# A six-layer attention stack: softmax work of layer 0 spread over slots, layer 1's projection started at the copies, the last slots laid out anew, and two layers' context matmuls in high and low halves

## What is computed

```python
# layer 0: 8 heads of 32
q, k, v = x @ Wq + bq, x @ Wk + bk, x @ Wv + bv
attn = softmax(where(adj == 0, -inf, q k^T / sqrt(32)))
x = layernorm(attn v @ Wo + bo + x) * gamma + beta
# layer 1: one head of 256
attn = softmax(where(adj == 0, -inf, (x Wq)(x Wk)^T / 16))
x = layernorm(x + (attn (x Wv)) @ Wo + bo) * gamma + beta
# layers 2 to 5: one head of 128
q, k = x Wq^T + bq, x Wk^T + bk
attn = softmax(where(adj == 0, -1e10, q k^T / sqrt(128)))
x = layernorm(x + (attn x) Wc^T) * gamma + beta
```

## Time and profile before

| what | value |
|---|---|
| median of 3 runs | 2371.49 us (2371.39 to 2374.79) |
| the profiled execution's own time | 2373.87 us |
| its span in the trace | 2372.1 us |
| PE busy | 2259.9 us, 95% |
| PE weight loads busy | 2136.2 us, 90% |
| DVE busy | 1783.3 us, 75% |
| ACT busy | 1620.0 us, 68% |
| POOL busy | 1794.9 us, 76% |
| granted PE clock, mean over the span | 0.99 of full speed |

### The profile page before, as it was taken

The page is one execution under the profiler, slowest core; times in us unless marked ns, Lnnn a source line. Parts: engine busy times, 40 slices in busy tenths (PEclk is TensorE's granted clock), DMA queues, the critical chain, the costliest instruction groups (busy, mean ns, idle before and its releaser), DMA issues.

```text
span 2372.1 us, 59576 instructions
## 1 busy us (share of the span) xinstructions
PE 2259.9 (95%) x20624; PEld 2136.2 (90%) x20624; DVE 1783.3 (75%) x7734; ACT 1620.0 (68%) x5515; POOL 1794.9 (76%) x2399
## 2 busy tenths in 40 slices
PE   6899999999999999999999999999999999999985
PEld 5799999999999999999999999999999999999974
DVE  4777777777877877877877877877777777777864
ACT  5667767767767767767767767766766766767742
POOL 3368878878878878878878878878878878878751
PEclk9999999999999999999999999999999999999998
DMA  4000000100110000010010000000010010000000
GB/s 154 20 23 24 30 28 24 30 28 25 29 28 25 29 28 26 28 28 26 28 28 27 27 28 28 26 28 28 26 28 28 26 28 28 26 29 17 15 10 14
DMA packets 38747, 68.78 MB, mean 29 GB/s; under 512 B 4400, under 2 KB 12848, under 8 KB 37936
## 3 DMA queue, kind: packets, MB, share of 16 engines
q1 hardware_dynamic: 38448, 64.97, 9.0%
HBM read 48.18 MB, written 16.78 MB: 27 GB/s over the span
## 4 chain that ended last, share of the span: by engine, by line
PE 80%; DVE 9%; ACT 7%; issue 2%; POOL 1%; DMA 0%; POOLq 0%; SPq 0%; DVEq 0%
PE value_bank L450 17%; PE qk_bank L442 16%; PE context_bank L595 9%; PE unit_bank L450 7%; PE unit_bank L442 7%; PE qk_bank L549 7%; PE score_bank L579 5%; ACT probs L676 5%; PE unit_bank L506 4%; PE unit_bank L518 3%; DVE scores L820 2%; PE score_bank L576 2%; PE score_bank L586 2%; DVE xT_lo L854 2%; DVE scores L860 1%
## 5 line engine op out<-in xcount | busy, mean ns | idle before, releaser
L1046 POOL TENSOR_TENSOR x<-y,rows 128x512 f32<-128x512 f32 x305 | 392.0, 1285 | 188.9 <-DVE y L913 188.9
L698 ACT CAST xT_hi<-qk_bank 128x512 fp32r<-128x512 f32 x320 | 187.7, 587 | 399.8 <-PE qk_bank L549 399.6
L676 ACT ACTIVATE probs<-scores,negmax 128x128 f32<-128x128 f32 x1024 | 399.1, 393 | 88.6 <-DVE negmax L820 88.6
L913 DVE TENSOR_SCALAR y<-y,mv,rstd 128x256 f32<-128x256 f32 x730 | 304.2, 459 | 191.6 <-POOL rstd L1030 191.3
L442 PE MATMUL qk_bank<-xT_hi,w_lo 128*128 128x256 f32 x1280 | 411.5, 321 | 21.6 <-DVE xT_lo L854 21.3
L1054 POOL TENSOR_TENSOR x<-x,rows 128x512 f32<-128x512 f32 x305 | 393.8, 1291 | 19.2
L450 PE MATMUL value_bank<-w_lo,xT_hi 128*128 128x256 f32 x1280 | 394.4, 308 | 0.0
L442 PE MATMUL qk_bank<-xT_lo,w_hi 128*128 128x256 f32 x1280 | 363.5, 284 | 0.0
L442 PE MATMUL qk_bank<-xT_hi,w_hi 128*128 128x256 f32 x1280 | 362.1, 283 | 0.0
L450 PE MATMUL value_bank<-w_hi,xT_lo 128*128 128x256 f32 x1280 | 361.8, 283 | 0.0
L450 PE MATMUL value_bank<-w_hi,xT_hi 128*128 128x256 f32 x1280 | 361.0, 282 | 0.0
(11 more groups left out here) (93 smaller groups left out, 6503.3 us busy)
## 6 DMA issues: line engine op xcount, KB each, us to landing
x0T<-xT_in SPq DMA_DIRECT2D x64, 256.0 KB, 3.0
x<-x_in SPq DMA_DIRECT2D x64, 256.0 KB, 3.0
out<-x_out SPq DMA_DIRECT2D x64, 256.0 KB, 2.3
adj<-adj_in SPq DMA_DIRECT2D x64, 128.0 KB, 2.2
late_weights<-w_in SPq DMA_DIRECT2D x2, 1024.0 KB, 7.1
rows<-rows_in SPq DMA_DIRECT2D x1, 1792.0 KB, 11.7
probs0T<-w_in SPq DMA_DIRECT2D x4, 256.0 KB, 4.2
x<-w_in SPq DMA_DIRECT2D x1, 1024.0 KB, 13.2
```

Of the source, the lines that this page charges most:

```text
L676: e = act.activation(probs0[:, j, g, quad], scores0[:, j, g, quad], ACT.Exp, scale=-1.0, bias=negmax0[:, j, g, quad:quad + 1], accum_out=t ...
L913: m = dve.tensor_scalar(y[:, r, g], y[:, r, g], mv[:, r, g, 0:1], rstd[:, r, g:g + 1], ALU.subtract, ALU.mult)
L1046: pool.tensor_tensor(result(norm), y[:, NORM_AT[norm] % YS], row_of_each(f"gamma{layer}"), ALU.mult).then_inc(zg_ready, 1)
```

## The change

1. Exponentials: unit 0's four activations are split, the first graph's before `move_qk` in phase 4, the second's after `move_probsT`. Unit 2 moves from the end of phase 0 to where unit 3 was in phase 1, unit 3 to the end of phase 1. DVE's `reciprocal0` and `row_max0(3)` move with them. POOL's and PE's orders stay.
2. Layer 1's projection has its own function: the eight products with `xT_hi` start once ACT's two copies are done, the four with `xT_lo` come last. They overwrite `qk_bank`, so `split_lo` of layer 1 reads `xT` in SBUF instead of `qk_bank`. It keeps its place in DVE's order except for three items at the end.
3. Layers 4 and 5: ACT writes `v_hi` and `probsT_hi`, DVE computes `v_lo` and `probsT_lo` (new `split_v`, 128x512, and `split_probsT`, 128x256), and the context is three fast products for each graph. PE waits for the low halves, before it reads them and before it overwrites `value_bank` and `score_bank`.
4. The last group's layers 3, 4 and 5 go from slots 323, 327, 331 to 322, 325, 328; group 62's layers 4 and 5 to 324 and 327. In slots 321, 324 and 327 DVE does `split_lo` later in its order.

```diff
-MOVED = {LAST_FIRST + 11: LAST_FIRST + 13}
+MOVED = {LAST_FIRST + 7: LAST_FIRST + 9, LAST_FIRST + 8: LAST_FIRST + 7, LAST_FIRST + 11: LAST_FIRST + 12,
+         LAST_FIRST + 12: LAST_FIRST + 10, LAST_FIRST + 16: LAST_FIRST + 13}
+FILL_IN = [LAST_FIRST + 6, LAST_FIRST + 9, LAST_FIRST + 12]
...
+def in_halves(i):
+    return item(i)[0] >= LAYERS - 2
...
+            def project_fused(i):
+                hi, lo = xT_hi[:, ring(i)], xT_lo[:, ring(i)]
+                pe.wait_ge(xT_ready, group + 1)
+                for n in range(KD):
+                    for kd in range(KD):
+                        for w in (w_lo, w_hi):
+                            pe.matmul(qk_bank[:, n * G * N:(n + 1) * G * N], split(w, "scores1", kd, n * P, n * P + P),
+                                      flat(hi[:, kd]), start=n == 0 and kd == 0 and w is w_lo, stop=False)
+                pe.wait_ge(xT_lo_ready, after(i))
+                for n in range(KD):
+                    for kd in range(KD):
+                        mm = pe.matmul(qk_bank[:, n * G * N:(n + 1) * G * N], split(w_hi, "scores1", kd, n * P, n * P + P),
+                                       flat(lo[:, kd]), start=False, stop=n == KD - 1 and kd == KD - 1)
...
             def context(i):
-                pe.wait_ge(probsT_ready, after(i))
-                pe.wait_ge(v_ready, after(i))
+                wait_probsT_moved(i)
+                wait_values_moved(i)
...
+                    for left, right in ((probsT_hi, v_lo), (probsT_hi, v_hi), (probsT_lo, v_hi)):
+                        mm = pe.matmul(context_bank[:, g * D:(g + 1) * D], left[:, ring(i), g], right[:, ring(i), g],
+                                       start=right is v_lo, stop=left is probsT_lo)
```

ACT's loop over the slots:

```diff
                 if (group := due(i, 6)) is not None:
-                    exp0(group, 0)
+                    exp0(group, 0, [0])
                 if (group := due(i, 5)) is not None:
                     exp0(group, 1)
                 if (group := due(i, 4)) is not None:
                     move_probs0T(group, 1)
-                    exp0(group, 3)
+                    exp0(group, 2)
...
                 if item(i - 1):
                     move_probsT(i - 1)
-                if (group := due(i, 5)) is not None:
-                    exp0(group, 2)
+                if (group := due(i, 6)) is not None:
+                    exp0(group, 0, [1])
+                if (group := due(i, 4)) is not None:
+                    exp0(group, 3)
```

DVE's functions and its loop over the slots:

```diff
             def split_lo(i):
+                source = qk_bank[:, :]
                 if layer == 1:
                     dve.wait_ge(xT_ready, group + 1)
+                    source = flat3(xT[:, :])
...
+            def split_probsT(i):
+                dve.wait_ge(probsT_hi_ready, IN_HALVES_AT[i] + 1)
+                dve.tensor_tensor(flat(probsT_lo[:, ring(i)]), score_bank[:, 0:G * N],
+                                  flat(probsT_hi[:, ring(i)]).bitcast(F32), ALU.subtract).then_inc(probsT_lo_ready, 1)
...
                 if item(i - 1):
                     row_max(i - 1)
-                if item(i):
+                if item(i) and not fills_in(i):
                     split_lo(i)
...
+                if item(i - 1) and in_halves(i - 1):
+                    split_v(i - 1)
...
-                if (group := due(i, 4)) is not None:
-                    reciprocal0(group, 2)
+                if (group := due(i, 3)) is not None:
+                    reciprocal0(group, 3)
...
+                if (group := due(i, 4)) is not None:
+                    reciprocal0(group, 2)
                     row_max0(group, 3)
...
                 if item(i - 2):
                     finish_or_normalise(("item", i - 2))
+                if item(i - 1) and in_halves(i - 1):
+                    split_probsT(i - 1)
                 if (group := due(i, 2)) is not None:
                     add_residual(("group", group))
```

More of the change, by code:

```diff
@@ L61, with fills_in @@
 LAST_FIRST = PERIOD * (GROUPS - 1)
-MOVED = {LAST_FIRST + 11: LAST_FIRST + 13}
+MOVED = {LAST_FIRST + 7: LAST_FIRST + 9, LAST_FIRST + 8: LAST_FIRST + 7, LAST_FIRST + 11: LAST_FIRST + 12,
+         LAST_FIRST + 12: LAST_FIRST + 10, LAST_FIRST + 16: LAST_FIRST + 13}
+PLACED = {slot: regular for regular, slot in MOVED.items()}
+FILL_IN = [LAST_FIRST + 6, LAST_FIRST + 9, LAST_FIRST + 12]
+def fills_in(i):
+    return i in FILL_IN
 def item(i):
-    if i in MOVED:
+    if i in MOVED and i not in PLACED:
         return None
-    for start, moved in MOVED.items():
-        i = start if i == moved else i
+    i = PLACED.get(i, i)
     layer = 1 if i % PERIOD == 0 else LAYERS - i % PERIOD
@@ L140 @@
 LATER_LEAD = 3
+def in_halves(i):
+    return item(i)[0] >= LAYERS - 2
+IN_HALVES_AT = {i: at for at, i in enumerate(i for i in ITEMS if in_halves(i))}
+IN_FULL_AT = {i: at for at, i in enumerate(i for i in ITEMS if not in_halves(i))}
 KEPT = [i for i in ITEMS if item(i)[0] > 1]
@@ L205, in gnn_stack @@
         v = sb("v", [RING, G, D])
+        v_hi = sb("v_hi", [RING, G, D], F32R)
+        v_lo = sb("v_lo", [RING, G, D], F32R)
+        probsT_hi = sb("probsT_hi", [RING, G, N], F32R)
+        probsT_lo = sb("probsT_lo", [RING, G, N], F32R)
         scores = sb("scores", [RING, G, N])
@@ L283, in gnn_stack @@
         v_ready = sem("v_ready")
+        v_hi_ready = sem("v_hi_ready")
+        v_lo_ready = sem("v_lo_ready")
         scores_in_psum = sem("scores_in_psum")
@@ L554, in project_qk, with wait_values_moved, wait_probsT_moved @@
                 layer, group = item(i)
-                parts = [("scores1", 0), ("scores1", P)] if layer == 1 else [(f"wqT{layer}", 0), (f"wkT{layer}", 0)]
                 pe.wait_ge(xT_lo_ready, after(i))
-                project(qk_bank, xT_hi[:, ring(i)], xT_lo[:, ring(i)], parts).then_inc(qk_in_psum, 1)
+                project(qk_bank, xT_hi[:, ring(i)], xT_lo[:, ring(i)],
+                        [(f"wqT{layer}", 0), (f"wkT{layer}", 0)]).then_inc(qk_in_psum, 1)
+            def project_fused(i):
+                layer, group = item(i)
+                hi, lo = xT_hi[:, ring(i)], xT_lo[:, ring(i)]
[10 more added lines that the diff above has]
+                                       flat(lo[:, kd]), start=False, stop=n == KD - 1 and kd == KD - 1)
+                mm.then_inc(qk_in_psum, 1)
+            def wait_values_moved(i):
+                if in_halves(i):
+                    pe.wait_ge(v_lo_ready, IN_HALVES_AT[i] + 1)
+                else:
+                    pe.wait_ge(v_ready, IN_FULL_AT[i] + 1)
+            def wait_probsT_moved(i):
+                if in_halves(i):
+                    pe.wait_ge(probsT_lo_ready, IN_HALVES_AT[i] + 1)
+                else:
+                    pe.wait_ge(probsT_ready, IN_FULL_AT[i] + 1)
             def project_v(i, g):
@@ L617, in _ @@
                     context(i - 2)
-                if item(i):
+                if item(i) and item(i)[0] == 1:
+                    project_fused(i)
+                elif item(i):
                     project_qk(i)
@@ L670, in move_k0, with exp0 @@
                 m.then_inc(k0_ready, 1)
-            def exp0(group, j):
+            def exp0(group, j, graphs=range(G)):
                 act.wait_ge(negmax0_ready, after_unit(group, j))
-                for g in range(G):
+                for g in graphs:
                     for quad in range(QUADS):
@@ L715, in move_v @@
                 act.wait_ge(v_in_psum, after(i))
-                act.copy(flat(v[:, ring(i)]), value_bank[:, :]).then_inc(v_ready, 1)
+                if NTH[i] >= RING:
+                    act.wait_ge(context_in_psum, after(i) - RING)
+                if in_halves(i):
+                    act.copy(flat(v_hi[:, ring(i)]), value_bank[:, :]).then_inc(v_hi_ready, 1)
+                else:
+                    act.copy(flat(v[:, ring(i)]), value_bank[:, :]).then_inc(v_ready, 1)
             def softmax(i):
@@ L726, in move_probsT @@
                 act.wait_ge(probsT_in_psum, after(i))
-                act.copy(flat(probsT[:, ring(i)]), score_bank[:, 0:G * N]).then_inc(probsT_ready, 1)
+                if in_halves(i):
+                    act.copy(flat(probsT_hi[:, ring(i)]), score_bank[:, 0:G * N]).then_inc(probsT_hi_ready, 1)
+                else:
+                    act.copy(flat(probsT[:, ring(i)]), score_bank[:, 0:G * N]).then_inc(probsT_ready, 1)
             def split_first(name):
@@ L976, in _ @@
                     reciprocal_total(i - 1)
+                if i + 1 == FILL_IN[0]:
+                    split_lo(i + 1)
+                if i in FILL_IN[1:]:
+                    split_lo(i)
                 if (group := due(i, 6)) is not None:
@@ L985, in _ @@
                     find_valid(group)
-                    reciprocal0(group, 3)
                 if (group := due(i, 8)) is not None:
```

21 lines of the change are left out of this document (15 added, 6 removed).

## The result

| what | before | after |
|---|---|---|
| median | 2372.53 us (2371.39 to 2374.79, 4 runs) | 2424.12 us (2423.15 to 2425.3, 4 runs) |
| span of the profiled execution | 2372.1 us | 2421.1 us |
| PE busy | 2259.9 us, 95% | 2254.6 us, 93% |
| DVE busy | 1783.3 us, 75% | 1945.4 us, 80% |
| a period in the middle, from phase 3 to phase 3 | 35.55 us | 36.35 us |

The ratio is 1.0216 with a 95% interval of 1.0199 to 1.0234: the changed kernel is 2.2% slower. 2415 had been forecast. Two executions stand far from the rest and are unexplained: one of ten of the kernel before beside the new end alone took 2405.23 us at a granted clock of 0.923, and one of seven of the new end alone took 12561.91 us and enters no ratio.

What follows compares the result with a forecast made beforehand. The prediction took the kernel as balanced between PE's chain and a DVE and POOL chain of nearly equal length. Periods +43.5, ramp +1.2, end -2 made +43 us, so 2415 us; forecast range 2395 to 2432 (0.60), stated range 2364 to 2432.

Steps and rivals of the forecast that it cites:

- The chain through DVE and POOL: Phase 3: split_v (+0.1) and split_probsT (0.38) on DVE make the layer-0 result on POOL 0.48 us later.
- The context in halves: PE, layers 4 and 5: six fast products replace a full context, gaining 0.13 to 0.16 us, twice a period.
- Exponentials, inside the whole change: Layer 1's transpose_x stops waiting for kT, waits for the layer-0 result, and gains 0.12 us, not 0.79.
- The collision: Layer 1's split_lo, both operands in SBUF, waits for POOL's scale; unit 0's normalisation starts 1.03 us later.
- PE at unit 1: PE's transposes of unit 1's probabilities wait for POOL and start 0.94 us later.
- Given back in phase 1: Context and twelve products in phase 1 no longer meet a late split_lo: 0.19 us a period back.
- The sum: Middle periods: +0.94 - 0.19 = +0.75 us each, bounds 0.6 to 1.0; 58 periods give +43.5.
- Ramp: First groups: later unit 2 exponential and unit 3 maximum cost about 1.2 us once, bounds 0 to 5.
- End: Last group: about +2 us for layers 4 and 5 each, -2 for each of three layers; -2, bounds -8 to +3.
- One reasoned step: At unit 1's transposes, POOL only 0.14 us ahead: a PE gain before them brings at most 0.1.
- Rival (b): POOL's chain has slack and PE's time counts: up to 1.1 us a period saved, 2307 or 2340; chance 0.17.
- the 0.21: Context in halves: gain if three passes replace four, a quarter off; the prediction went by the row's 0.15 instead.

Runs made afterwards that it cites:

- the new end alone: The kernel before with only the new slots at the end (MOVED, FILL_IN and the late split_lo): 2368.56 us, ratio 0.9962 (0.9922 to 1.0002).

## Why the prediction was right, and where it was not

The forecast was the likeliest case and its mechanism is what the runs show. It put the whole at +43 us; the profiled executions differ by 49. Point by point:

- **The chain through DVE and POOL.** Right. From the context at 1216.51, `shift` of the layer-0 result ends at 11.35 (1226.58 + 1.28); before it was 10.95. Forecast +0.48, measured 0.41 on average. `split_probsT` was put at 0.38 between bounds of 0.31 and 0.44: the next operation starts 0.34 after it, and it takes 0.42.
- **The context in halves.** Context and the twelve products behind it take 1218.66 − 1216.51 = 2.15, 2.27 before: 0.12, and 0.13 on average, against 0.13 to 0.16.
- **Exponentials, inside the whole change.** `transpose_x` was put 0.12 earlier and waiting for `x`: it waits for `x`, and is 0.19 earlier.
- **The collision.** Right in kind, place and size: `scale` over the split, 1.57 in the period shown, an end 0.55 after POOL's; unit 0 of layer 0 starts 0.96 later, 1.03 was forecast. POOL's wait for the reciprocal: 0.71 against 0.7.
- **PE at unit 1.** 0.88 later, against 0.94. Both are a little smaller than forecast because `scale`, behind which the split ends, is 0.41 later on average and not 0.48.
- **Given back in phase 1.** Right in place, mis-sized: context and products take 1239.21 − 1236.92 = 2.29 instead of 2.46, so 0.17 came back there. But ahead of it the transposes, which now follow POOL, take 1236.92 − 1236.43 = 0.49 instead of 0.43, and 0.11 is left; 0.19 was forecast. This miss and the one before it, 0.08 and 0.06, have opposite signs in the sum and cancel.
- **The sum.** +0.80 a period against +0.75. The forecast's 35.60 + 0.75 = 36.35 is what was measured, though partly by luck: the one period it started from was one of the longer ones, and the mean is 35.55. 57 periods at 0.80 are 45.5.
- **Ramp.** Not confirmed: +1.2 forecast, −0.9 measured, and two executions of the same ramp differ by 0.8 at other granted clocks, so one pair of executions cannot show it.
- **End.** Wrong: −2 forecast, bounds −8 to +3; measured +4.3, of which 1.7 are the two longer periods. The new slots alone gave −5.7. The halves alone cost 10.9 in the old end; with new slots they cost 8 to 10 (after's 186.8 or the 186.6 without the projection, against 176.8 for the slots alone). The two terms fared differently. "−2 for each of three layers", −6, is about what the new slots give, though no run shows whether for the reasons stated. "+2 for layers 4 and 5 each", +4, was really 8 to 10. Layer 5 alone costs 4.4 in the old end. Where the rest goes is in part argued: the one place shown costs 1.8, and an item in halves stands behind a neighbour's normalise in more places than the last group's.

One reasoned step fell, though the sum stood. The prediction said that a gain on PE's side before the unit-1 transposes can bring at most 0.1, since POOL was only 0.14 ahead. The exponentials alone brought 0.33 a period. The 0.14 was read rightly; wrong was to treat POOL's time as fixed. Part of its chain waits for PE a slot earlier, so both moved: layer 1's split on DVE stands ahead of PE's projection as well as of POOL's unit 0. That PE passes unit 1's transposes without waiting for POOL would have said that PE's own path had the last word there. In the whole change this does not show, because the halves lengthen the chain that `x` comes by, and the blocked split lies behind it. Rival (b), that PE's time counts, was right in part: alone, the exponentials brought 0.33 of the 0.6 that PE's side had to give, and with layer 5's halves 0.52. What stopped it there was not POOL's lead but the normalise and the row maximum ahead of the split on DVE.

The parts do not add. One by one, in us a period: exponentials −0.33, halves +0.38, early projection +0.35, which is +0.40; together +0.80. (By the medians the parts are −21.1, +33.3, +25.4 and −5.4 for the new end, 32.2 us of the 51.6; the rest is 0.34 a period.) The traces show where it comes from. As long as layer 1 projects in the old order, the period follows the start of that projection, which waits for `xT_lo`: counted from the phase-3 context 14.13 before, 13.79 with the exponentials, 13.62 with layer 5's halves as well, 14.58 with both layers' halves, 14.67 with the split reading `xT`, for periods of 35.55, 35.23, 35.03, 35.94 and 36.09. With the early projection it follows POOL instead. PE's unit-1 transposes, counted from the context in phase 3, come at 19.07 before; at 18.73 with the exponentials and at 18.57 with layer 5's halves as well; at 19.53 with the projection, and at 19.37 with the projection, exponentials and layer 5's halves. So, if beside the projection layer 5's halves are still worth their 0.16, the exponentials are worth nothing: their 0.34 came by way of an earlier `kT`, `xT` and split, and with the projection the split ends 0.55 after POOL's `scale` whenever its input is there; `scale` itself starts at 12.79 with the exponentials as without. That alone is most of the 0.40. It is worked out and not measured: exponentials and projection without any halves were not run.

## What to carry to other kernels

Before giving an instruction on DVE a second operand in SBUF, look at what POOL does at that very moment in the timeline. The price is not the instruction's but the rest of POOL's, and then whatever is queued behind it on DVE. Where two chains run within 0.2 us of each other, take the changes apart: here the exponentials were worth 0.33 us a period and layer 5's halves 0.20, and layer 4's halves and the projection took 0.55 and 0.76 away again (the projection by itself 0.35), in one change that was read as one. And do not take an engine's lead as fixed: follow it back to what set it.

## What the runs showed of the hardware

- The blocking works in both directions: DVE's 0.69 split becomes 1.2 to 1.57 when POOL's 128x512 operation has begun before it, and in all middle periods of the five kernels with it ends 0.54 to 0.55 after POOL's, whether it began 0.25 or 0.6 after it; when DVE's wins, POOL's 128x256 operation takes 0.44 more (1.06 instead of 0.62) and ends 0.47 after DVE's.
- Two SBUF operands alone cost next to nothing: 0.692 against 0.684 with one of them in PSUM.
- A full float32 context costs only a little more than three fast products: a pair of graphs gains 0.13 on average out of the prediction's 0.83, and not the 0.21 that it set beside its own term.
